# The first row of a transformer kernel: four steps of its attention in another order, and two activation tables loaded at other places

## The reference

```python
def attention_block(x):                       # x: 16 x 512 x 256
    h = layernorm(x) * g1 + b1
    q, k, v = split(h @ qkv_w + qkv_b)        # 16 heads of 16
    # each token attends to 15 neighbours, 7 to each side
    scores = einsum(q, windows(k)) / 4
    x = x + (softmax(scores) @ windows(v)) @ proj_w + proj_b
    m = layernorm(x) * g2 + b2
    return x + gelu_exact(m @ fc1_w + fc1_b) @ fc2_w + fc2_b      # 256 -> 1024 -> 256

x = x + attention_block(layernorm(x))
z = layernorm(x)
main = gelu_tanh(z @ W1m + b1m) @ W2m + b2m
top2, gate = top_2(softmax(mean_over_tokens(z) @ w_gate + b_gate))   # of 8 experts, per row
x = x + a * main + (1 - a) * sum(gate[e] * expert_mlp(z, e) for e in top2)
```

## Time and profile before

| what | value |
|---|---|
| median of 3 runs | 1946.28 us (1944.24 to 1946.32) |
| profiled execution, its own time | 1946.44 us |
| span of that execution, first to last instruction | 1944.7 us |
| mean granted TensorE clock | 0.998 |
| PE busy | 1916.3 us (99%) |
| DVE busy | 1392.7 us (72%) |
| ACT busy | 1191.7 us (61%) |
| POOL busy | 855.9 us (44%) |

### The profile page before, as it was taken

How to read it: one execution, slowest core, us unless ns; L and a number is a source line. 1 busy time by engine, 2 the same in 40 slices (tenths; PEclk the granted TensorE clock), 3 DMA queues, 4 the chain that set the end, 5 groups by cost and what they waited for, 6 DMA issues and landing times.

```text
span 1944.7 us, 57593 instructions
## 1 busy us (share of the span) xinstructions
PE 1916.3 (99%) x23696; PEld 1727.3 (89%) x23696; DVE 1392.7 (72%) x2331; ACT 1191.7 (61%) x1867; POOL 855.9 (44%) x784
## 2 busy tenths in 40 slices
PE   7899999999999999999999999999999999999999
PEld 6789889898998989899888998989999898998998
DVE  7576776867767687777867768687686877768744
ACT  5575665756657566575755657566575665757554
POOL 3537254362534626245271543625346252452725
PEclk9999999999999999999999999999999999999999
DMA  3121210312112121121311203121021311212111
GB/s 113 55 75 55 68 52 23 91 50 82 49 30 82 42 85 48 42 77 32 86 56 54 65 23 91 50 76 55 26 83 45 85 46 41 78 34 86 45 61 55
DMA packets 147342, 116.25 MB, mean 60 GB/s; under 512 B 17836, under 2 KB 139912, under 8 KB 147080
## 3 DMA queue, kind: packets, MB, share of 16 engines
q1 hardware_dynamic: 146504, 111.78, 19.7%
q10 hardware_dynamic: 576, 0.79, 0.1%
HBM read 85.52 MB, written 8.39 MB: 48 GB/s over the span
## 4 chain that ended last, share of the span: by engine, by line
PE 96%; DVE 2%; ACT 1%; issue 1%; POOL 0%; SPq 0%; DMA 0%; ACTq 0%; POOLq 0%; DVEq 0%
PE psB L236 56%; PE psA L236 27%; PE psA L1137 4%; PE psA L1100 3%; PE psA L1112 3%; PE psA L1013 2%; PE psA L1154 0%; DVE hr_lo L544 0%; DVE zT_lo L568 0%; ACT qm L883 0%; DVE pr L625 0%; DVE pr L634 0%; ACT hr_hi L854 0%; DMA pT<-in_L_attn_norm_b 0%; DVE smax L623 0%
## 5 line engine op out<-in xcount | busy, mean ns | idle before, releaser
L544 DVE TENSOR_TENSOR hr_lo<-hf,hr_hi 128x512 fp32r<-128x512 f32 x512 | 476.6, 931 | 457.0 <-ACT hr_hi L854 456.5
L444 POOL TENSOR_SCALAR wx_hi<-raw 128x512 fp32r<-128x512 f32 x256 | 201.6, 787 | 715.6 <-DMA raw<-in_L_ffn_W2e 379.2
L854 ACT ACTIVATE hr_hi<-hf 128x512 fp32r<-128x512 f32 x512 | 324.1, 633 | 277.3 <-PE psB L236 189.2
L446 POOL TENSOR_TENSOR wx_lo<-raw,wx_hi 128x512 fp32r<-128x512 f32 x256 | 398.4, 1556 | 21.4
L236 PE MATMUL psB<-wx_hi,hr_hi 128*128 128x256 f32 x1024 | 287.5, 281 | 0.7 <-DVE hr_lo L544 0.6
L236 PE MATMUL psB<-wx_hi,hr_lo 128*128 128x256 f32 x1024 | 286.4, 280 | 0.0
L236 PE MATMUL psB<-wx_lo,hr_hi 128*128 128x256 f32 x1024 | 285.7, 279 | 0.0
L850 ACT ACTIVATE hf<-psB,b1x 128x512 f32<-128x512 f32 x256 | 175.3, 685 | 167.3 <-PE psB L236 166.2
L236 PE MATMUL psB<-z_hi,wx_hi 128*128 128x512 f32 x512 | 211.9, 414 | 0.0
L236 PE MATMUL psB<-z_hi,wx_lo 128*128 128x512 f32 x512 | 202.7, 396 | 0.4 <-issue 0.4
L236 PEld LDWEIGHTS psB<-wx_hi,hr_hi 128*128 128x128 f32 x1024 | 192.5, 188 | 10.5 <-DVE hr_lo L544 1.3
(11 more groups left out here) (159 smaller groups left out, 4777.5 us busy)
## 6 DMA issues: line engine op xcount, KB each, us to landing
raw<-in_L_ffn_W1e SPq DMA_DIRECT2D x256, 128.0 KB, 2.2
raw<-in_L_ffn_W2e SPq DMA_DIRECT2D x256, 128.0 KB, 2.2
vb<-vs SPq DMA_DIRECT2D x64, 144.0 KB
out_x<-acc SPq DMA_DIRECT2D x32, 256.0 KB, 2.2
vb<-vs SPq DMA_DIRECT2D x64, 120.0 KB
xin<-in_L_attn_x SPq DMA_DIRECT2D x15, 512.0 KB, 3.7
tm<-in_L_ffn_b2e SPq DMA_DIRECT2D x32, 128.0 KB, 3.0
raw<-in_L_attn_fc_w SPq DMA_DIRECT2D x8, 256.0 KB, 4.5
```

Source lines behind the costliest of these rows:

```text
L444: g.tensor_scalar(wx[0][:, s, :], raw[:, s, :], 1.0, 0.0, ALU.mult, ALU.add).then_inc(w_hi.sem, 1)
L446: g.tensor_tensor(wx[1][:, s, :], raw[:, s, :], wx[0][:, s, :].bitcast(f32), ALU.subtract).then_inc(w_lo.sem, 1)
L544: v.tensor_tensor(hr[1][:, c % 2, :], hf[:, c % 3, :], hr[0][:, c % 2, :].bitcast(f32), ALU.subtract).then_inc(h_lo.sem, 1)
L854: a.activation(hr[0][:, c % 2, :], hf[:, c % 3, :], ACT.Copy).then_inc(h_hi.sem, 1)
```

## The change

It touches only what happens once, in the opening and at t = 0:

1. PE turns the normed row first and the small rows behind it. DVE copies `smallT` after three of the four low parts, not ahead of them. `warm(6)` becomes `warm(7)`.
2. `shifts(0)` is done after `values(0, 0)`.
3. `scores(0, 3)` stands ahead of `attend(0, 0)`: PE does `turn(1)`, `scores(3)`, `attend(0)`, `attend(1)`.
4. `turn(0, 3)` stands ahead of `attend(0, 2)`.
5. The table of the tanh form of GELU is no longer loaded in the opening; the table of GELU is loaded in slot 16 ahead of `gained_T` in place of slot 19; the tanh table is loaded in slot 31 behind the query blocks of row 1, ahead of `z3`, in place of slot 27.
6. `WARM` has fewer products: 18 to 14 in slot 3, slots 7 and 11 none, 12 to 4 in slot 8.

```diff
             for n in range(FIRST):
+                if n == FIRST - 1:
+                    v.wait_ge(small_ps.sem, 1)
+                    v.tensor_copy(smallT[:, :], psA[:, 3, 0:NSM]).then_inc(small_t.sem, 1)
...
             gained_T(0, tr1, t1_f1, t1_hi, t1_lo, 1, oG1, oB1)
-            shifts(0)
...
             values(0, 0)
+            shifts(0)
...
-            table(ACT.Gelu_apprx_tanh)
             gained_T(0, tr1, t1_f0, t1_f1, t1_hi, 0, oG1, oB1)
...
                     elif q == 16:
                         a.wait_ge(proj.sem, proj.all(t))
+                        if t == 0:
+                            table(ACT.Gelu)
                         gained_T(t, tr2, t2_f0, t2_f1, t2_hi, 0, oG2, oB2)
-                    elif q == SPLIT - 1:
+                    elif q == SPLIT - 1 and t:
                         table(ACT.Gelu)
...
-                    elif q == SPLIT + 7:
+                    elif q == SPLIT + 7 and t:
                         table(ACT.Gelu_apprx_tanh)
...
                         query_blocks(t + 1, 1)
+                        if t == 0:
+                            table(ACT.Gelu_apprx_tanh)
...
-            WARM = {3: 18, 4: 4, 7: 4, 8: 12, 10: 3, 11: 4, 12: 8, 14: 12, 16: 8}
+            WARM = {3: 14, 4: 4, 8: 4, 10: 3, 12: 8, 14: 12, 16: 8}
+            pe.wait_ge(consts.sem, 4)
             pe.wait_ge(z1_s.sem, z1_s.all(0))
             for c in range(KD):
                 transposes(tr1, c, tn, c)
+            pe.wait_ge(small_in.sem, small_in.all(0))
+            pe.transpose(psA[:, 3, 0:NSM], small[:, :], ident[0:NSM, 0:NSM]).then_inc(small_ps.sem, 1)
...
                     elif q == 6:
-                        attend(t, 0)
+                        if t:
+                            attend(t, 0)
                         turn(t, 1)
                     elif q == 7:
                         scores(t, 3)
+                        if t == 0:
+                            attend(t, 0)
...
                     elif q == 11:
+                        if t == 0:
+                            turn(t, 3)
                         attend(t, 2)
-                        turn(t, 3)
+                        if t:
+                            turn(t, 3)
```

7 lines of the change are left out of this document (1 added, 6 removed).

## The result

| | before | changed |
|---|---|---|
| median of the runs | 1946.3 us (6 runs, 1944.24 to 1948.63) | 1955.89 us (6 runs, 1953.67 to 1961.4) |
| ratio | | 1.0052, 95% interval 1.0038 to 1.0066 |
| profiled execution | 1946.44 us, span 1944.7 | 1953.67 us, span 1951.9 |
| mean granted clock | 0.998 | 0.996 |

The kernel is slower by half a per cent, 9.6 us, where 6.6 less were forecast. To see where, I take the time of the router's `MAX8` on DVE, which comes once in each row: in the profiled execution of before it stands at 103.37 us for row 0 and the later rows take 1770.1 us up to that of row 15; now it is 104.52 and 1776.2. So the profiled difference of 7.2 us is 1.1 in row 0 and 6.1 in rows that no edit touches. Both are against the forecast.

The account below looks back on a forecast made before the run. Only row 0's chain in the first 105 us was taken to matter, PE being full afterwards. Terms -0.6, -5.25, -1.88 and +1.2 sum to -6.5 us: 1939.7 us forecast, overall range 1937.0 to 1943.5.

Parts of the forecast that it names:

- Opening: Row 0's start: turning the normed row first brings the first QKV product forward, -0.6 us, bounds 0 and -0.8.
- shifts: `shifts(0)` moved behind `values(0, 0)` on DVE, its POOL result off the chain: 0, bound +0.2 us.
- first exp without its load: Row 0's first exp: ACT gets 1.28 us, but DVE is busy and covers it: 0.
- scores(3) ahead of attend(0): Row 0 attention: `mask(3)` starts at 35.15, not 41.00, and the gain carries through to `attend(2)`: -5.25 us.
- turn(3) ahead of attend(2): Row 0 attention: the turn fills PE's wait for DVE's low parts: -1.88 us, bounds -1.2 and -2.2.
- code arriving late behind weight loads: Explanation of PE's 1.91 us issue wait inside `attend(0)`, where the DMA engines were 0.78 busy.
- Weights: POOL's low parts of the weights, queued among the attention steps, have 4.27 us of rest before the norm: charged 0.
- GELU table: Load moved ahead of `gained_T` in slot 16, where ACT idles; nothing gained at the old place: 0 at both ends.
- tanh table: Load moved ahead of `z3`, unhidden there, 0.23 returned at the old place: +1.2 us, bounds -0.2 and +1.5.
- the drain of the rival: At the moved tanh load: a drain of about 1.38 us beside the load, giving 1941.0 us; chance 0.06.
- The stall or the low clock stays: Row 0 attention: 1.9 us for the stall, 1.7 for the clock remain, giving 1941.4 to 1943.3; chance 0.14.
- The slower rival: Row 0's first MLP at 1.2 GHz after fewer warm products: 1961 us for all of it, 1950 for half; chance 0.05.

Follow-up runs that it names:

- b_open: Kernel before with only the normed row turned first, `shifts(0)` after `values(0, 0)` and no table load in the opening: 1945.97 us, ratio 1.0000.
- b_sc3: Kernel before with only the fourth scores moved ahead of the first products with V, all warm products kept: 1946.85 us, ratio 1.0000.
- b_turn3: Kernel before with only the fourth turn moved ahead of the third products: 1947.51 us, ratio 1.0001.
- rate2: Kernel before plus, behind its last chunk on PE alone, a dense run of short products and a spaced one: dense blocks 3.5 to 4.0 us start to start.
- u_gelu: Changed kernel with the GELU table load back in slot 19: 1953.22 us, ratio 1.0034 to the kernel before.
- b_open_gelu: Kernel before with the turned opening, no table load in it, and the GELU table loaded ahead of `gained_T` in slot 16: 1947.97 us, ratio 1.0010.
- u_turn3: Changed kernel with the fourth turn behind the third products again: 1955.71 us, ratio 1.0041 to the kernel before.
- b_phase: Kernel before with 218 unused PE instructions in the idle opening, putting later code borders where the changed kernel has them: 1951.91 us, ratio 1.0025.
- b_warm: Kernel before with only the 20 warm products of row 0 taken away: 1951.32 us, ratio 1.0023.
- u_tanh: Changed kernel with the tanh table loaded in slot 27 again: 1955.23 us, ratio 1.0039 to the kernel before.
- pad_tanh: Changed kernel with 19 unused transposes in the idle opening and the tanh table back at its old place: 1951.64 us, ratio 1.0025 to the kernel before.
- pad19: Changed kernel with 19 unused transposes on PE in the idle opening, restoring its instruction count: 1953.34 us, ratio 1.0033 to the kernel before.
- b_moves: Kernel before with the opening turned and the fourth scores and fourth turn moved, tables and warm products as before: 1947.37 us, ratio 1.0008.

## Why the prediction was wrong

- *Opening*, -0.6 forecast: right, 0.78 by the trace. In the median it is not to be told from nothing (`b_open` 1.0000, 0.9990 to 1.0009).
- *shifts* and *first exp without its load*, 0: nothing in the trace speaks against it.
- *scores(3) ahead of attend(0)*, -5.25: **the step that failed.** `mask(3)` came at 35.13 as worked out, but "what `mask(3)` gains carries through to `attend(2)`" is wrong. DVE did carry it, 6.6 us of it up to its last low part at 43.79. But PE was no longer behind DVE. `attend(0)` and `attend(1)` stand together and are cut by two waits for code, 1.66 and 2.12; `attend(1)` ends at 41.70, not at 37.8; the clock falls at 39.95, inside the second wait; `turn(2)` is at 43.51 and `attend(2)` at 47.60. The sum took one stall of 1.91, "moved along" to near the end of `scores(3)`. By count of the records a border does lie there, at about 34.8, and nothing stopped; it was the next two, one block each further on, that did. The sum should have priced blocks of 256 short instructions at about 3.5 us each. `b_sc3` measures the term: 0, between -1.8 and +1.9 us by its interval.
- *turn(3) ahead of attend(2)*, -1.88: failed by the same cause. `attend(3)` does follow `attend(2)` directly, and the two have two waits inside, 1.42 and 2.41. `b_turn3` measures 0, between -1.8 and +1.9. A gain of up to 1.8 us from either alone is not excluded; the -5.25 is, and the -1.88 only just.
- *The reading behind both*, "code arriving late behind weight loads": refuted by the first wait at a DMA share of 0.00 and by `rate2`. In before the code packet ahead of the wait starts at 33.03, and PE goes on 2.39 us later at a DMA share of 0.78; ahead of the first wait of the changed kernel it is 2.64 at 0.00. The bound "one more issue gap" came from it; there were three more.
- *Weights*, 0, and *GELU table*, 0 at both ends: row 0 shows no loss. But the GELU load together with the missing load of the opening takes three records from ACT's list and so makes the stops of rows 8 and 12, 3.5 us of gaps. The prediction put both at 0 for what they do where they stand and did not ask what they do to the place of everything behind them. `u_gelu` stands 6.8 us above its before, the changed kernel 9.6, with intervals that overlap; the pair alone (`b_open_gelu`) measures +1.9 us, between 0 and +3.7.
- *tanh table*, +1.2: right for the load; `z_hi` stands at 102.38 where it stood at 101.18, and PE waits 1.4 for it. Not foreseen: the clock is at its lower level from 104.8 for 3.4 us, behind 3.50 us (100.90 to 104.40) in which PE was busy 1.76, and row 1 takes 1.0 longer. `u_turn3` and `u_gelu` show that this need not follow from the load's place. No second wait as long as the load, the drain of the rival, is to be seen: from the load's start to `z_hi` it is 1.40 us.
- *Rivals.* "The stall or the low clock stays" named the right place and less than half of its size: 1.9 for the stall and 1.7 for the clock, where the waits alone are 5.5 us more than before. Of the sign of being wrong, "an issue gap inside `scores(3)`" did not come, "a granted clock of 0.50 anywhere from 30 to 60" did. The slower rival, a low clock in the first MLP, did not happen: the kernel is slower, as it said, for another reason. The clock was low from 39.9 to 46.8 and from 53.6 to 57.0 and back before the MLP.
- *What no step held*: that 19 products without use, taken away in row 0, move the code borders of fifteen later rows. The prediction said that no edit touches that part and that row 0 "moves it as a block". `b_phase` shows 4.6 us from moving the borders alone, `b_warm` 4.2. In the profiled execution of the changed kernel the 6.1 us of the later rows are about 3.3 for rows 8 and 12, 1.0 for the clock in row 1, and the rest, under 2, for the borders; in `u_gelu` it is 2.5. The runs don't split the whole more finely: the parts measured alone (0, 0, +4.2, 0 and, for the tanh table, about 1.7 by `u_tanh` and `pad_tanh`, not clear of noise) leave some 3 to 4 of the 9.6 us, of which the pair of table edits may be 1.9.

## What to carry to other kernels

Where a wait is put down to "issue", count the instructions between such waits before giving it a cause. On PE they stood 256 apart, and short matmuls (here 0.010 us) went no faster than one such block per 3.45 us from stop to stop; bunching them only lengthens the waits, and enough long matmuls between them (a block of 3.9 us in `rate2`) hide the fetch. In an unrolled program every instruction added or removed early moves the code borders of everything behind it: try the same change with its count made up in an idle stretch (`pad19`, `b_phase`) before believing that a part is touched or untouched. The same goes for ACT, where three records fewer were enough. One profiled execution can flatter a kernel: `b_moves` was 2.9 us under before in its profile and not below it in the median.

## What the runs showed of the hardware

- PE stops for code only where a multiple of 256 of its records ends (all stops over 0.25 us in twenty traces, after the first 20 us). Its next block starts 3.47 to 4.03 us after the one before when the work in it is shorter, with nothing else running. At about 3.9 us of work a block there was no stop (the spaced run of `rate2`). In row 0 the 16384-byte packet starts at 35.28, 39.02, 47.60 and 51.42, and PE goes on 2.64, 2.35, 2.45 and 2.35 us later.
- ACT waits about 0.28 us longer at record 63 of a group of 128: so in 76 of 228 instructions at that place in eighteen traces, and in at most 4 at any other place.
- The same 128 matmuls take 1.28 us at the full clock and 1.93 at the lower one. In `rate2` the clock stays at its lower level through 22 us in which PE works 11.92, and returns in the spaced run, where it works without a pause.
- A DVE instruction of 0.69 us takes 1.68 when it begins 0.16 us behind POOL's and beside it, while POOL's takes 1.74 when DVE goes first and 1.30 when POOL does. A shift of 0.28 us on a third engine decides which. In the trace of before the medians are 0.69 and 1.73 us in 156 pairs with DVE first, 1.55 and 1.30 in 52 with POOL first.
